# Delta rule on one core: query norms from VectorE block transposes and SBUF transfers, and a single buffer for the decay rows

## The reference, cut to what matters

```python
mixed = silu(causal_conv1d(hidden @ w_qkv, conv_w))     # kernel size 4
q, k, v = split(mixed)
q = q * rsqrt(sum(q * q, -1) + 1e-6)                    # per token and head
k = k * rsqrt(sum(k * k, -1) + 1e-6)
# per token, with decay exp(g) and step size beta:
#   St = St * exp(g); delta = (v - k St) * beta; St = St + k delta; o = q St
core = core * rsqrt(mean(core * core, -1) + 1e-6) * norm_weight * silu(z)
```

## Time and profile before

| what | value |
|---|---|
| median of 3 runs | 3333.22 us (3330.68 to 3338.06) |
| the profiled execution's own time | 3335.47 us |
| its span | 3333.6 us |
| TensorE busy | 3238.8 us, 97% |
| VectorE busy | 2414.8 us, 72% |
| GpSimd busy | 1863.5 us, 56% |
| ScalarE busy | 1541.4 us, 46% |
| granted TensorE clock, mean | 0.991 |

### The profile page before, as it was taken

How to read it: one execution, slowest core, us unless ns; L and a number is a source line. 1 busy time by engine, 2 the same in 40 slices (tenths; PEclk the granted TensorE clock), 3 DMA queues, 4 the chain that set the end, 5 groups by cost and what they waited for, 6 DMA issues and landing times. The chain is left out here.

```text
span 3333.6 us, 59535 instructions
## 1 busy us (share of the span) xinstructions
PE 3238.8 (97%) x20832; PEld 2152.7 (65%) x20832; DVE 2414.8 (72%) x3622; ACT 1541.4 (46%) x4983; POOL 1863.5 (56%) x1824
## 2 busy tenths in 40 slices
PE   5899999999999999999999999999988999999999
PEld 2577777777777777777777777777764444454444
DVE  6799999999999999999999999999940011034453
ACT  2455556555655555556555655565631000011232
POOL 2677777777777777777777777777740000011132
PEclk8999999999999999999999999999989999999999
DMA  2122322323232323322332233223215222211001
GB/s 101 42 61 77 70 71 58 77 64 71 64 77 64 71 65 71 73 65 61 78 71 69 58 78 67 67 66 77 75 52 211 76 101 101 76 38 64 0 13 38
DMA packets 373958, 231.85 MB, mean 70 GB/s; under 512 B 290304, under 2 KB 323200, under 8 KB 368128
## 3 DMA queue, kind: packets, MB, share of 16 engines
q1 hardware_dynamic: 372368, 220.97, 25.4%
q10 hardware_dynamic: 1296, 7.08, 0.5%
HBM read 156.39 MB, written 71.57 MB: 68 GB/s over the span
## 5 line engine op out<-in xcount | busy, mean ns | idle before, releaser
L722 PE MATMUL acc<-xT,wc 128*128 128x512 f32 x2048 | 935.8, 600 | 2.8 <-PEq L111 2.0
L722 PEld LDWEIGHTS acc<-xT,wc 128*128 128x128 f32 x2048 | 370.2, 191 | 373.2 <-issue 372.5
L1007 DVE SCALAR_TENSOR_TENSOR d_conv<-acc,wc,d_conv 128x511 f32<-128x511 f32 (+2 forms) x768 | 567.0, 738 | 42.7 <-ACT d_conv L1176 33.5
L735 PE MATMUL acc<-wc,xT 128*128 128x256 f32 x2048 | 473.4, 384 | 0.0
L735 PEld LDWEIGHTS acc<-wc,xT 128*128 128x128 f32 x2048 | 379.1, 190 | 46.2
L622 POOL TENSOR_TENSOR d_bf<-d_kks,d_gam 128x512 f32<-128x512 f32 x128 | 160.3, 1273 | 317.9 <-ACT d_kks L1222 317.9
L1530 PE MATMUL acc<-t_area 128*128 128x512 f32 x768 | 332.5, 592 | 1.0 <-ACT t_area L1979 1.0
L1035 DVE STREAM_TRANSPOSE d_em<-d_dm 128x1024 f16<-128x1024 f16 x256 | 314.5, 1229 | 2.2
L2036 POOL TENSOR_SCALAR t_veps<-t_mv 128x1 f32<-128x1 f32 x32 | 9.7, 303 | 546.1 <-DVE t_mv L1775 546.1
L1042 DVE TENSOR_TENSOR d_zm<-d_tz,cons 128x512 f16<-128x512 f32 x384 | 259.1, 675 | 52.7 <-PE d_tz L790 47.7
L1765 DVE TENSOR_TENSOR t_x<-acc,t_x 128x512 f32<-128x512 f32 x16 | 11.1, 692 | 392.4 <-PE acc L1530 392.4
(11 more groups left out here) (227 smaller groups left out, 7084.5 us busy)
## 6 DMA issues: line engine op xcount, KB each, us to landing
d_decay<-decay_rows SPq DMA_DIRECT2D x64, 512.0 KB, 5.2
v_rows<-d_vb SPq DMA_DIRECT2D x256, 128.0 KB, 2.3
d_vn<-v_rows SPq DMA_DIRECT2D x64, 512.0 KB, 3.6
core_rows<-d_ob SPq DMA_DIRECT2D x1024, 32.0 KB, 1.7
t_area<-core_rows SPq DMA_DIRECT2D x30, 1024.0 KB, 4.8
wc<-in_w SPq DMA_DIRECT2D x96, 256.0 KB, 3.3
t_x<-in_x SPq DMA_DIRECT2D x4, 1024.0 KB, 9.6
t_area<-in_wout ACTq DMA_DIRECT2D x2, 2048.0 KB, 13.4
```

The source lines that it names most:

```text
L722: last = nc.tensor.matmul(bank(TILE[j])[:, :], wtile(j, k), xT[:, k, r % B * S:(r % B + 1) * S], start=k == 0, stop=k == KT - 1)
L735: last = nc.tensor.matmul(bank(f"z{j}")[:, i * GV * P:(i + 1) * GV * P].rearrange("p (h n) -> p h n", h=GV), xT[:, k, r % B * S + (2 * j + ...
L1007: nc.vector.scalar_tensor_tensor(c[:, d:S], bank(TILE[j])[:, 0:S - d], tap(j, KS - 1 - d), c[:, d:S], ALU.mult, ALU.add).then_inc(taps, 1)
```

## The change

The query turn leaves TensorE. A new `flip_q` transposes `qT` on VectorE in 32 x 32 blocks into the SBUF tile `qf`, at the end of the slot, ahead of `level_e(m, 4)`. A new `move_q` on SP, last in its slot, moves the 16 block groups to their places in `qn` by 16 transfers from SBUF to SBUF. `q_square` and `q_norm` work from `qn` one slot later, in the `recur` part; `o_norm` waits for `eq` explicitly. The two decay buffers become one, and `load_decay` for the next unit waits for the scans of the current unit and moves behind the four weight loads at the head of SP's slot. `flip_q` shares the semaphore `v_flipped` with `flip_v`, which is counted by two now.

```diff
+MOVED = 16 * NC * NC
-        cb, decay, ident = many("conv", 2, [P, S]), many("decay", 2, [P, GV, S]), sb("ident", [P, S])
+        cb, decay, ident = many("conv", 2, [P, S]), sb("decay", [P, GV, S]), sb("ident", [P, S])
+        qf, qn = sb("qf", [P, NC, NC, 32]), sb("qn", [P, NC, NC, 32])
-        RING_ORDER = ("q", "k", "z1", "v1", "k_turn", "z0", "kq", "v0", "khat_turn", "q_turn", "kk")
+        RING_ORDER = ("q", "k", "z1", "v1", "k_turn", "z0", "kq", "v0", "khat_turn", "kk")
...
         def _(sp):
...
-                wait(sp, gam_ready, at(back(n, 2), GV, GV))
-                sp.dma_start(decay[n[1] % 2][:, :, :], bc(src, P, 0)).then_inc(decay_loaded[n[1] % 2], 16)
+                wait(sp, gam_ready, at(back(n, 1), GV, GV))
+                sp.dma_start(decay[:, :, :], bc(src, P, 0)).then_inc(decay_loaded, 16)
...
             def slot(n, project, invert, recur, finish):
-                if n[0] * ROUND + n[1] < ITERS - 1:
-                    load_decay((n[0], n[1] + 1))
                 if invert:
                     next_weights(back(n, 1), 1)
                 if project:
                     next_weights(n, 0)
                 if invert:
                     next_weights(back(n, 1), TILES)
                 if project:
                     next_weights(n, 3)
+                if n[0] * ROUND + n[1] < ITERS - 1:
+                    load_decay((n[0], n[1] + 1))
                 if invert:
                     store_v(back(n, 1))
...
                 if project:
                     next_weights(n, 2)
+                if invert:
+                    move_q(back(n, 1))
...
+            def move_q(m):
+                sp.wait_ge(v_flipped, at(m, 2, 2))
+                wait(sp, q_squares, at(back(m, 1), NC, NC))
+                for a in range(NC):
+                    for b in range(NC):
+                        sp.dma_start(qn[b * 32:(b + 1) * 32, a].rearrange("p c j -> p (c j)"),
+                                     qf[a * 32:(a + 1) * 32, b].rearrange("p c j -> p (c j)")).then_inc(q_moved, 16)
...
         def _(pool):
...
             def o_norm(s):
                 pool.wait_ge(o_squares, at(s, GV * NC, GV * NC))
+                pool.wait_ge(eq_ready, count(s))
...
                 if invert:
-                    q_norm(m)
                     decayed_keys(m, 1)
+                if recur:
+                    q_norm(s)
...
         def _(pe):
...
-            def q_turn(n):
-                pe.wait_ge(silued, nth(n, "silued", 1))
-                ring_free(n, "q_turn")
-                turn(bank("q_turn"), qT[third(n)], q_turned)
...
                     level_z(m, 3)
-                    q_turn(m)
...
         def _(dve):
...
+            def flip_q(m):
+                dve.wait_ge(silued, nth(m, "silued", 1))
+                wait(dve, q_moved, at(back(m, 1), MOVED, MOVED))
+                nc.vector.transpose(qf[:, :, :, :], qT[third(m)][:, :].rearrange("p (c b j) -> p b c j", c=NC, b=NC)).then_inc(v_flipped, 1)
...
                     convolve(n, 2, 3)
                 if invert:
+                    flip_q(m)
                     level_e(m, 4)
...
         def _(act):
...
             def q_square(n):
-                act.wait_ge(q_turned, count(n))
+                act.wait_ge(q_moved, at(n, MOVED, MOVED))
                 wait(act, eq_ready, count(n, 1))
-                wait(act, k_squares, min(at(back(n, -1), NC, NC), NC * ITERS))
-                squares(bank("q_turn"), 0, qss, q_squares, scale=(RMS_EPS * HD) ** 0.5)
+                squares(lambda c: qn[:, :, c, :], lambda c: qn[:, :, c, :], qss, q_squares, scale=(RMS_EPS * HD) ** 0.5)
...
-                if invert:
-                    q_square(m)
-                if recur:
+                if recur:
+                    q_square(s)
                     solved(s, 2)
```

More of the change, by code:

```diff
@@ L350, in delta_rule @@
         z_projected, z_silued = sem("z_projected"), sem("z_silued")
-        tab_ready, decay_loaded, gam_ready, gamc_ready, gams_ready = sem("tab_ready"), sems("decay_loaded"), sem("gam_ready"), sem("gamc_ready"), sem("gams_ready")
+        tab_ready, decay_loaded, gam_ready, gamc_ready, gams_ready = sem("tab_ready"), sem("decay_loaded"), sem("gam_ready"), sem("gamc_ready"), sem("gams_ready")
         k_turned, k_squares, rk_ready = sem("k_turned"), sem("k_squares"), sem("rk_ready")
         khat_ready, khat_turned, kT_ready, ks_ready = sem("khat_ready"), sem("khat_turned"), sem("kT_ready"), sem("ks_ready")
-        q_turned, q_squares, eq_ready = sem("q_turned"), sem("q_squares"), sem("eq_ready")
+        q_moved, q_squares, eq_ready = sem("q_moved"), sem("q_squares"), sem("eq_ready")
         kk_done, bf_ready, bh_ready, bl_ready = sem("kk_done"), sem("bf_ready"), sem("bh_ready"), sem("bl_ready")
@@ L428, in per_token @@
             return bc(ap, P, 2)
-        RING_ORDER = ("q", "k", "z1", "v1", "k_turn", "z0", "kq", "v0", "khat_turn", "q_turn", "kk")
-        RING_BANK = {"q": 1, "k": 2, "z1": 0, "v1": 1, "k_turn": 2, "z0": 0, "kq": 2, "v0": 0, "khat_turn": 2, "q_turn": 2, "kk": 1}
+        RING_ORDER = ("q", "k", "z1", "v1", "k_turn", "z0", "kq", "v0", "khat_turn", "kk")
+        RING_BANK = {"q": 1, "k": 2, "z1": 0, "v1": 1, "k_turn": 2, "z0": 0, "kq": 2, "v0": 0, "khat_turn": 2, "kk": 1}
         RING_FREED = {"k": (taps, "taps", 2), "q": (taps, "taps", 5), "v0": (taps, "taps", 8), "v1": (taps, "taps", 11),
                       "z0": (z_silued, "z_silued", 0), "z1": (z_silued, "z_silued", 1),
-                      "k_turn": (khat_ready, "squares", NC - 1), "khat_turn": (kT_ready, "once", 0), "q_turn": (q_squares, "squares", NC - 1),
+                      "k_turn": (khat_ready, "squares", NC - 1), "khat_turn": (kT_ready, "once", 0),
                       "kk": (kk_copied, "once", 0), "kq": (kqs_ready, "once", 0)}
@@ L446, in delta_rule @@
                     "zr_ready": (1, 2), "closed": (2, 1), "tt_ready": (2, 1)}
-        RING_LAG = {"q": 1, "k": 0, "z1": 2, "v1": 0, "k_turn": 0, "z0": 2, "kq": 1, "v0": 0, "khat_turn": 0, "q_turn": 1, "kk": 0}
+        RING_LAG = {"q": 1, "k": 0, "z1": 2, "v1": 0, "k_turn": 0, "z0": 2, "kq": 1, "v0": 0, "khat_turn": 0, "kk": 0}
         CONV_LAG = {"k": 0, "v1": 0, "v0": 0, "q": 0}
@@ L536, in store_v @@
             def store_v(m):
-                sp.wait_ge(v_flipped, count(m))
+                sp.wait_ge(v_flipped, at(m, 2, 1))
                 wait(sp, v_moved, at(back(m, 1), 80, 80))
@@ L1013, in decays @@
                 q, r = n
-                dve.wait_ge(decay_loaded[r % 2], q * (ROUND * 8) + (r // 2 * 16 + 16))
+                dve.wait_ge(decay_loaded, at(n, 16, 16))
                 wait(dve, bf_ready, nth(n, "bf_ready", h, 1))
-                nc.vector.tensor_tensor_scan(gam[h][:, :], decay[r % 2][:, h, :], ident[:, :], 0.0, ALU.mult, ALU.add).then_inc(gam_ready, 1)
+                nc.vector.tensor_tensor_scan(gam[h][:, :], decay[:, h, :], ident[:, :], 0.0, ALU.mult, ALU.add).then_inc(gam_ready, 1)
             def flip_v(m):
@@ L1182, in silu @@
                 if j >= 2:
-                    wait(act, v_flipped, count(n, 1))
+                    wait(act, v_flipped, at(back(n, 1), 2, 1))
                 v = vraw
@@ L1191, in z_silu, with squares @@
                 nc.scalar.activation(sz[m[1] % 2][:, 2 * h:2 * h + 2, :], bank(f"z{h}")[:, :].rearrange("p (c n) -> p c n", c=2), ACT.Silu).then_inc(z_silued, 1)
-            def squares(src, spare, dst, sem_, scale=1.0):
+            def squares(src, out, dst, sem_, scale=1.0):
                 for c in range(NC):
-                    nc.scalar.activation(junk[:, spare + c, :], chunk(src, c), ACT.Square, scale=scale,
-                                         accum_out=dst[:, c:c + 1]).then_inc(sem_, 1)
+                    nc.scalar.activation(out(c), src(c), ACT.Square, scale=scale, accum_out=dst[:, c:c + 1]).then_inc(sem_, 1)
             def k_square(n):
@@ L1200, in k_square @@
                 wait(act, rk_ready, at(back(n, 1), 2, 1))
-                wait(act, q_squares, at(back(n, 2), NC, NC))
-                squares(bank("k_turn"), 0, kss, k_squares)
+                wait(act, k_squares, at(back(n, 1), NC, NC))
+                squares(lambda c: chunk(bank("k_turn"), c), lambda c: junk[:, c, :], kss, k_squares)
             def q_square(n):
-                act.wait_ge(q_turned, count(n))
+                act.wait_ge(q_moved, at(n, MOVED, MOVED))
                 wait(act, eq_ready, count(n, 1))
-                wait(act, k_squares, min(at(back(n, -1), NC, NC), NC * ITERS))
-                squares(bank("q_turn"), 0, qss, q_squares, scale=(RMS_EPS * HD) ** 0.5)
+                squares(lambda c: qn[:, :, c, :], lambda c: qn[:, :, c, :], qss, q_squares, scale=(RMS_EPS * HD) ** 0.5)
             def copy_kT(n):
```

## The result

| | before | changed |
|---|---|---|
| median of the runs | 3331.95 us (4 runs) | 3449.15 us (4 runs, 3446.70 to 3449.89) |
| profiled execution | 3335.47 us, span 3333.6 | 3449.83 us, span 3448.0 |
| mean granted TensorE clock | 0.991 | 0.973 |

The ratio is 1.0347, with a 95% interval of 1.0329 to 1.0365. The direction was the forecast one; the size was not, 117 us where 55 were expected.

What follows compares the result with a forecast made beforehand. TensorE, busy 398.6 of 400 us in the delta rule, was taken as the bound. 72 us lost less 17 saved gave +55 on the profiled 3335.47 us, 3390, so a median of 3388 us, range 3350 to 3410.

Steps and rivals of the forecast that it cites:

- Step 1: Query transposes leave TensorE: slot keeps 0.26 of 0.47 us, the read then waiting for VectorE's state; 17 us saved.
- Steps 2, 3 and 4: VectorE's query transpose; ScalarE's squares, the norms and PSUM; one buffer for the decay rows: each claimed to cost nothing.
- Step 5: Sixteen moves on SP's queue make taps 4.8 us late in 15 group-first slots: 72 us lost, bounds 15 and 93.
- the faster rival: The transfers cost no time where the taps are wanted, leaving only TensorE's saving: 3303 to 3316 us; chance 0.08.
- the even one: Moves issue in 0.33 to 0.40 us, taps 1 to 2 us late: 3318 to 3346 us; chance 0.09.
- the one with a wait in every slot: The flip isn't covered and VectorE's 0.65 us comes on top in each slot: 42 us more, 3430 us; chance 0.05.

Runs made afterwards that it cites:

- eight moves ahead: Changed kernel with eight of the sixteen query moves ahead of the tap load on SP's queue and eight behind it: 3360.15 us, 1.0085 of the kernel before.
- moves to memory: Changed kernel with the sixteen moves going to memory and squares summed over the unmoved blocks, leaving query norms wrong: 3409.32 us in one run.
- moves behind: Changed kernel with all sixteen moves behind the tap load, at the head of SP's next slot: 3311.78 us, 0.9941 of the kernel before.
- four moves ahead: Changed kernel with four of the sixteen moves ahead of the tap load and twelve behind it: 3311.63 us, 0.9933 of the kernel before.

## Why the prediction was right or wrong

- **Step 1** held in its sum and in the wait that comes last: 0.29 us per slot against 0.26, 18 us against 17, and the read starts 0.05 us behind the state. But the step had TensorE reach the read 0.16 us before the state's end and stand there for 0.21 us. TensorE was slower than that, since the growth takes 0.55 us and not 0.45 without the turn ahead of it; the wait is 0.05 us. That the price of the new order fell almost wholly into the wait was luck.
- **Steps 2, 3 and 4** held: nothing for the flip (0.70 us instead of some 0.65), the squares, the norms and the decay buffer. The version without the turn and nothing in its place is no faster than the one with everything but the bad order.
- **Step 5** had the mechanism and the place right and its size wrong. I took "the pace is that of the sequencer" from stores to memory, 0.48 us each; with both ends in SBUF it is 0.63, so sixteen take 10.0 us and not 7.7. The taps came 6.9 us later and not 4.8: 2.3 us more for the pace, the landing behind the weights as taken (0.75 us for 0.7), the pauses a little less (some 0.4 us on average for 0.7). Together 103 us where I had 72, beyond even the upper bound of 93: I had bounded the pace only on the side of a quicker issue, by the lone one of 0.33 us, and had taken the nearest row as if it were the ceiling. The break-even of the faster rival was off too: issues of 0.34 us in a row leave out the step's own later landing, and with its 0.7 us they would have had to take 0.29.
- **A term was missing altogether**: I let TensorE's wait count one for one and never asked what the engine does after it. The clock's fall adds 34 us. The profile page of before had a hint: in its first slice, where TensorE waits, the clock stands at 8 tenths. I read it only for the busy middle.
- **The rule of the Trainium skill** ("DMA: Bandwidth & Descriptors", "Issuing engines are not separate DMA queues") that issue time is usually small relative to the transfer doesn't hold here: a move takes 1.8 us from issue to landing in the profile page's DMA part beside 0.59 us for its issue, and sixteen issues take 10 us of the queue. Step 5 was right not to lean on it. The rival that did is out, and so are the even one and the one with a wait in every slot.

In numbers: -18 + 103 + 34 = +119 in the delta rule, against -17 + 72 = +55.

## What to carry to other kernels

Transfers that nobody is waiting for still delay what stands behind them on their queue: before adding any, list what that queue must issue next in every kind of slot, the rare ones too, and put the load that is due first ahead of them. A small table that is reloaded in place ties its load to the last use of the old one; 128 bytes per partition for two more buffers took that load off the path and made the order on the queue harmless. And the price of a wait on TensorE is more than its length, since the clock may fall after it.

## What the runs showed of the hardware

- Issuing a transfer with both ends in SBUF took 0.59 us on SP's queue, the same 16 KB to memory 0.42 us.
- In 6 of the 15 series of moves at a group's start the sixteen took 0.7 to 1.2 us longer, as if one issue had taken 1.3 to 1.8 us instead of 0.59. Stores have such pauses, before the change too (9.41 us for sixteen instead of 7.70); their cause wasn't looked for.
- The four f32 products of the state's growth (L872, before) took 0.53 us to the next start behind half-precision products and 0.45 behind f32 ones.
- TensorE's clock was at 1.2 GHz for 3.4 us at the end of 10 of 15 idle stretches of 1.8 to 3.0 us or just behind it (eight moves ahead), and for 6.8 or 10.2 us around each of those of 6.9 to 8.2 us, where it fell while the engine still stood idle. It fell in all 15 of 4.0 to 5.4 us (moves to memory) and in none of 0.2 to 1.4 us (before, moves behind, four moves ahead). A stretch of 3.00 us was seen without a fall and one of 1.85 us with one. A fall of 3.4 us cost 1.6 us.
